# The down product in three products of halves, for 46 chunks of the last five expert stages

## The chip, the core and the metric

The kernel runs on one core of a Trainium2 chip. The metric is the device time of one execution in microseconds, as the median of several runs; lower is better. A core has TensorE (PE in the profile; its weight loads are PEld), VectorE (DVE), ScalarE (ACT), GpSimd (POOL) and SyncE (SP), which here issues all DMAs. Each engine works through its own queue in the order in which the program issues it; semaphores tie the queues together.

## The reference

Four rows of 1024 tokens with 128 features pass four residual sublayers: a gated linear attention (sublayer 1), a mixture of experts (MoE), a windowed softmax attention over 64 keys, and the same mixture of experts again. The part that the change touches is the MoE:

```python
logits = x @ gate_w.T                    # x: layernormed, 128 features
probs = softmax(logits)                  # 32 experts, top 8 of them, renormalised: comb
for each expert e:                       # 64 hidden features each
    g, u = split(x @ gate_up_w[e].T)
    out += (u * silu(g)) @ down_w[e].T * comb[:, e]
```

## The kernel before, in words

**Stages and chunks.** The MoE of 512 tokens is one stage. There are 16 stages: four rows, twice two halves (f is 0 or 1 for the first MoE, 2 or 3 for the second). A stage goes through the 32 experts in 16 chunks of two experts, 128 hidden features by 512 tokens each. The list SCHEDULE has the order of the stages and of the softmax attentions between them; a place in it has a name ("first", "second", ...). In this text the last five stages are called A, B, C, D and E, and the chunk 13 of stage A is A13:

- A is (row 2, f 2), place "second"; B is (3, 1), "third"; then half an attention; C is (2, 3), "fourth"; the other half; D is (3, 2), "second"; E is (3, 3), "fourth", the last. The stage ahead of A is (3, 0), "first".

**A chunk on the engines.** TensorE makes the gate product (three products of halves, float32r: hi x hi, hi x lo, lo x hi; lines 1489 to 1491) and then the up product in the same way, each into a PSUM bank of its own. ScalarE takes the silu of the gate bank into a tile of `work` (line 1030). VectorE multiplies it with the up bank, into the same tile (1270; "mul" below). GpSimd multiplies it with the tokens' weights for these two experts (847; "weigh"), which a DMA has spread over the partitions in `spread_w`. TensorE then adds the float32 product with the down weights to one bank (1512; "down"); the profile counts it as two matmuls.

**Order.** In slot s of a stage TensorE issues gate_up(s), down(s - 3) (LAG is 3), then the steps that a plan (PLAN, SPECIAL) names for the slot. ScalarE issues silu(s) and the slot's steps, VectorE mul(s) and the steps, GpSimd weigh(s) and the steps. The steps belong to other parts of the work: norms (m_stats and s_stats on VectorE, m_rstd and s_rstd on GpSimd, m_apply and s_apply on ScalarE), the transpose and its halves (moe_turn, z_hi, z_lo), the router (route and r_sum, top, weigh's exponentials on ScalarE, comb, cnorm, weighT), keys, queries, values, y_back, proj.

**Banks.** Gate and up products use three banks each, in the order of RINGS (line 378). A product waits until the chunk that last used its bank is done with it: the gate product for silu, the up product for mul. In stages that stand alone or in pairs behind an attention the ring has places where the bank comes back after two chunks instead of three: [0, 1, 2, 1, 2, 0, 1, 2, 0, 1, 2, 1, 2, 0, 1, 2] in C; in D and E positions 12 and 13 take the banks of 10 and 11.

**Weights.** `weighT` in slot 13 ends a stage's router work for the next one; ScalarE copies the result, SyncE sends it to DRAM and spreads it back by quarters of four chunks (two DMAs each) into the two halves of spread_w; the first waits for this chain, later ones for GpSimd to be done with the quarter two before.

Of the kernel before, what the change touches and what calls it, by code (L numbers as in the profile page):

```python
# [27 lines left out]
P = 128  # L28
# [32 lines left out]
HOOKS = 3  # L61
HALF_BLOCKS = NB * HG // 2
# [14 lines left out]
def own(*steps):  # L77
    return [(name, n, 0) for name, n in steps]


def back(*steps):
# [199 lines left out]
    },  # L281
    (ROWS - 1, "third"): {
# [88 lines left out]
for _, stage_place, stage_row, stage_part in SCHEDULE:  # L371
# [3 lines left out]
    else:  # L375
# [3 lines left out]
         48: [0, 1, 2] * 16, 64: ([0, 1, 2] * 6 + [1, 2]) * 2 + [0, 1, 2] * 8}  # L379
STARTS = [k for k, part in enumerate(SEGMENT) if k == 0 or SEGMENT[k - 1] != part]  # L380
# [40 lines left out]
def hybrid_block(nc, x, wqkv_a, lam, g1, g2, g3, w1, w2, wqkv_b, wout, bout, wgate, wg, wu, wd, out):  # L421
# [3 lines left out]
    with ExitStack() as ctx:  # L425
# [3 lines left out]
        def sem(name):  # L429
# [31 lines left out]
        qkv = sb("qkv", [P, T, 3 * D])  # L461
        elu = sb("elu", [P, T, 2 * D])
        kv_terms, w_terms = sb("kv_terms", [P, 2, HD * HD * H]), sb("w_terms", [P, H * HD * HD])
        kv = sb("kv", [P, HD * HD])
        attn, squares = sb("attn", [P, G, T, D]), sb("squares", [P, T, D])
# [3 lines left out]
        gain = sb("gain", [P, T, D])  # L469
# [25 lines left out]

        bank = [ctx.enter_context(nc.psum_tensor(f"bank{i}", [P, 512], F32))[:] for i in range(8)]
# [22 lines left out]
            sem("kv_terms_ready"), sem("kv_summed"), sem("w_terms_ready"), sem("attn_summed"))  # L519
        squared, tok_summed, head_gain, head_scaled = (  # L520
# [202 lines left out]
        def _(pool):  # L723
# [115 lines left out]
            def hidden(row, f, s):  # L839
                n = chunk(row, f, s)  # L840
                if n < EACH:
                    pool.wait_ge(spread_first[n], 32)
                elif s % EACH == 0:
                    k = n // EACH
                    pool.wait_ge(spread_loaded[k % 2], 32 * ((k + 1) // 2))
                pool.wait_ge(gated_ready, n + 1)
                pool.tensor_tensor(work[:, n % WORK], work[:, n % WORK],  # L847
                                   spread_w[:, n // EACH % 2, s % EACH], ALU.mult).then_inc(hid_gated, 1)
# [38 lines left out]
        def _(act):  # L887
# [147 lines left out]
            steps = {"x_apply": lambda row, n: norm_apply(row, "x", n), "m_apply": lambda row, n: norm_apply(row, "m", n),  # L1035
# [23 lines left out]
            for period, place, row, f in SCHEDULE:  # L1059
                if place not in PARTS:  # L1060
                    for s in range(CH):
                        if s == LAG and not starts_stream(row, f):
                            y_copy(STAGE_AT[row, f] - 1)
                        if s >= (1 if STAGE_AT[row, f] else FIRST) or not starts_stream(row, f):
                            silu(row, f, s)
                        run_steps(steps, period, place, s)
                else:
                    exponentials(row, f[0], 0)
                    exponentials(row, f[0], 1)
                    end, drain = END_AT[row, f[0]], HOOKS * (f[1] - f[0])  # L1070
# [20 lines left out]
        def _(dve):  # L1091
# [181 lines left out]
            steps = {"x_stats": lambda row, n: norm_stats(row, "x", n), "m_stats": lambda row, n: norm_stats(row, "m", n),  # L1273
# [84 lines left out]
        def _(pe):  # L1358
# [109 lines left out]
            def gate_up(row, f, s):  # L1468
# [10 lines left out]
                for w_hi, w_lo, banks, freed, ready in ((gate_hi, gate_lo, GATE_BANKS, silu_ready, gate_ready),  # L1479
                                                        (up_hi, up_lo, UP_BANKS, gated_ready, up_ready)):  # L1480
                    if there is not None:
# [22 lines left out]
            def down(n):  # L1504
                (row, f), c = STREAM[n // CH], n % CH
                pe.wait_ge(hid_gated, n + 1)
# [5 lines left out]
                pe.matmul(bank[Y_BANK], down_w[:, c], work[:, n % WORK], start=(c == 0),  # L1512
                          stop=(c == CH - 1)).then_inc(down_done, 1)
# [133 lines left out]
```

## Time and profile before

| | us |
|---|---|
| timed runs | 1011.54, 1008.63, 1011.01 |
| median | 1011.01 |
| profiled execution | 1018.66 |
| its span, first to last instruction | 1016.9 |
| mean granted TensorE clock | 0.956 |

The profile tells of one execution. Its span is the time from the first instruction to the last, and the rows give times in us from its start. "Busy" is the time in which an engine executes; a matmul's end is modelled, and matmuls that follow each other overlap in the rows, so that their pace is the distance between two starts. In a timeline a row has start, duration, engine, line, operation, what it writes and reads, the shape, how many were merged, and, in brackets, how long the engine had been idle and what released it.

### The profile page before, as it was taken

Reading aid. Unit: us, or ns where it says so; the run is one execution under the profiler, and the core shown is the slowest. Engines: PE = TensorE matmul, PEld = TensorE weight load, DVE = VectorE, ACT = ScalarE, POOL = GpSimd, SP = SyncE. Lnnn points to the kernel's source line nnn. Section 1 sums busy time; section 2 is a strip of 40 time slices with the busy share of each in tenths; the row PEclk is TensorE's granted clock in tenths of the full one; section 3 lists DMA queues with packets and bytes.
Section 4 is the critical chain, followed back from the end, with each engine's and each line's share of the span. In section 5 each row is a group of like instructions: output and inputs, shape, how many; then the busy total and the mean of one; then the engine's idle time right before and its main releaser. Section 6 shows DMA issues by size and latency. Waiting matters only on the chain.

```text
span 1016.9 us, 16679 instructions
## 1 busy us (share of the span) xinstructions
PE 917.2 (90%) x5472; PEld 629.8 (62%) x5472; DVE 643.8 (63%) x1447; ACT 612.5 (60%) x1876; POOL 660.4 (65%) x610
## 2 busy tenths in 40 slices
PE   2366999899999999899999899999999998998998
PEld 1144656676666666587666556677666566666665
DVE  4877865687759647688739636778744247447432
ACT  4444756984664576876674566698465458376432
POOL 6676967566778749556759746756665446545654
PEclk8558999999999999979999999999999999999999
DMA  5004361114453544510433544530344661260362
GB/s 181 0 1 97 82 127 44 43 44 101 92 125 85 128 92 90 132 38 17 94 85 86 124 90 89 124 83 17 70 100 86 125 142 39 63 147 13 83 127 62
DMA packets 63320, 85.67 MB, mean 84 GB/s; under 512 B 3777, under 2 KB 29186, under 8 KB 62978
## 3 DMA queue, kind: packets, MB, share of 16 engines
q1 hardware_dynamic: 63234, 84.61, 36.8%
q8 instruction: 43, 0.70, 0.3%
q14 instruction: 43, 0.35, 0.1%
HBM read 79.32 MB, written 5.28 MB: 83 GB/s over the span
## 4 chain that ended last, share of the span: by engine, by line
PE 58%; ACT 14%; POOL 8%; DVE 7%; issue 5%; DMA 1%; DVEq 0%; SPq 0%; ACTq 0%; POOLq 0%
PE bank L1512 16%; PE bank L1489 8%; PE bank L1491 8%; PE bank L1490 8%; ACT probs L1055 6%; PE bank L1533 3%; POOL work L847 3%; PE bank L1548 3%; PE bank L1562 2%; POOL kv_terms L812 2%; ACT work L1030 1%; PE bank L1526 1%; POOL probs L855 1%; PE bank L1372 1%; PE bank L1366 1%
## 5 line engine op out<-in xcount | busy, mean ns | idle before, releaser
L847 POOL TENSOR_TENSOR work<-work,spread_w 128x512 f32<-128x512 f32 x256 | 338.3, 1333 | 179.8 <-DVE work L1270 155.6
L1270 DVE TENSOR_TENSOR work<-work,bank 128x512 f32<-128x512 f32 x256 | 174.4, 682 | 227.9 <-ACT work L1030 143.3
L1512 PE MATMUL bank<-work,down_w 128*128 128x512 f32 x512 | 266.1, 604 | 14.2 <-POOL work L847 9.1
L1030 ACT ACTIVATE work<-bank 128x512 f32<-128x512 f32 x256 | 150.9, 595 | 182.3 <-PE bank L1491 179.3
L1055 ACT ACTIVATE probs<-bank,neg_max 128x96 f32<-128x96 f32 x512 | 166.0, 383 | 12.3 <-DVE neg_max L1298 6.5
L1489 PE MATMUL bank<-z_hi,gate_hi 128*128 128x512 f32 x256 | 169.0, 660 | 2.5 <-ACT work L1030 1.8
L855 POOL TENSOR_TENSOR probs<-probs,prob_inv 128x768 f32<-128x768 f32 x64 | 94.1, 1470 | 73.0 <-DVE prob_inv L1306 73.0
L1055 ACT ACTIVATION_READ_ACCUMULATOR probs<-bank,neg_max 128x1 f32 x512 | 126.8, 250 | 0.0
L1512 PEld LDWEIGHTS bank<-work,down_w 128*128 128x128 f32 x512 | 95.6, 191 | 44.4 <-POOL work L847 14.5
L1491 PE MATMUL bank<-z_hi,gate_lo 128*128 128x512 f32 x256 | 102.1, 399 | 0.0
L1491 PE MATMUL bank<-z_hi,up_lo 128*128 128x512 f32 x256 | 101.8, 398 | 0.0
L1489 PE MATMUL bank<-z_hi,up_hi 128*128 128x512 f32 x256 | 101.8, 398 | 0.0
L1490 PE MATMUL bank<-z_lo,gate_hi 128*128 128x512 f32 x256 | 101.6, 397 | 0.0
L1490 PE MATMUL bank<-z_lo,up_hi 128*128 128x512 f32 x256 | 100.9, 394 | 0.0
L812 POOL TENSOR_TENSOR kv_terms<-elu,qkv 128x1024 f32<-128x1024 f32 x32 | 81.6, 2553 | 17.9 <-DVE elu L1127 14.8
L1312 DVE COPY probsT<-bank 96x512 f32<-96x512 f32 x128 | 80.3, 666 | 5.0 <-PE bank L1548 4.7
L1298 DVE TENSOR_REDUCE neg_max<-bank 128x4 f32<-128x384 f32 x128 | 64.9, 548 | 24.7 <-PE bank L1533 23.7
L1548 PE MATMUL bank<-ident,probs 128*96 128x128 f32 x512 | 71.4, 282 | 10.2 <-DVE probsT L1312 8.4
L1489 PEld LDWEIGHTS bank<-z_hi,gate_hi 128*128 128x128 f32 x256 | 49.1, 192 | 40.2 <-issue 30.5
L1533 PE MATMUL bank<-keysT,qm 32*128 32x96 f32 x1024 | 70.7, 273 | 0.0
L1490 PEld LDWEIGHTS bank<-z_lo,gate_hi 128*128 128x128 f32 x256 | 49.3, 193 | 34.1 <-issue 31.3
L1548 PEld LDWEIGHTS bank<-ident,probs 128*96 128x96 f32 x512 | 54.2, 128 | 23.0 <-issue 13.3
(154 smaller groups left out, 1481.0 us busy)
## 6 DMA issues: line engine op xcount, KB each, us to landing
spread_w<-comb_dram SPq DMA_DIRECT2D x126, 512.0 KB, 6.7
vals<-v_dram SPq DMA_DIRECT2D x16, 384.0 KB, 4.0
x_buf<-x SPq DMA_DIRECT2D x8, 256.0 KB, 3.2
v_dram<-v_tok SPq DMA_DIRECT2D x8, 256.0 KB, 5.0
out<-xs SPq DMA_DIRECT2D x8, 256.0 KB, 4.2
spread_w<-wg SPq DMA_DIRECT2D x1, 1024.0 KB, 7.2
spread_w<-wu SPq DMA_DIRECT2D x1, 1024.0 KB, 9.3
comb_dram<-combT SPq DMA_DIRECT2D x16, 64.0 KB, 1.6
```

The source lines that it names most:

```text
L812: pool.tensor_tensor(kv_terms[:, i % 2].rearrange("p (e d h) -> p e d h", e=HD, d=HD), k.unsqueeze(2).broadcast_to([P, HD, HD, H]), v.unsq ...
L847: pool.tensor_tensor(work[:, n % WORK], work[:, n % WORK], spread_w[:, n // EACH % 2, s % EACH], ALU.mult).then_inc(hid_gated, 1)
L855: pool.tensor_tensor(pr, pr, prob_inv[:, i % 2, part].unsqueeze(2).broadcast_to([P, HALF_BLOCKS, KW]), ALU.mult).then_inc(probs_normed, 1)
L1030: act.activation(work[:, n % WORK], bank[GATE_BANKS[ring_of(row, f, s)]], ACT.Silu).then_inc(silu_ready, 1)
L1055: a = act.activation(probs[:, i % 2, m], bank[hg][:, b * KW:(b + 1) * KW], ACT.Exp, bias=neg_max[:, i % 2, m:m + 1], accum_out=prob_sum[:, ...
L1270: dve.tensor_tensor(work[:, n % WORK], work[:, n % WORK], bank[UP_BANKS[ring_of(row, f, s)]], ALU.mult).then_inc(gated_ready, 1)
L1489: pe.matmul(dst, w_hi[:, cols], h, start=True, stop=False)
L1490: pe.matmul(dst, w_hi[:, cols], l, start=False, stop=False)
L1491: pe.matmul(dst, w_lo[:, cols], h, start=False, stop=True).then_inc(ready, 1)
L1512: pe.matmul(bank[Y_BANK], down_w[:, c], work[:, n % WORK], start=(c == 0), stop=(c == CH - 1)).then_inc(down_done, 1)
L1533: mm = pe.matmul(bank[hg][:, KW * b:KW * (b + 1)], qm[feats, i // T, NB * (i % T) + b].rearrange("p j q -> p (j q)"), keysT[feats, first:f ...
L1548: mm = pe.transpose(bank[4 + b % 2][0:KW, P * hg:P * (hg + 1)], probs[:, i % 2, hg * NB + b], ident[:])
```

## The change

For 46 chunks in A to E (table PARTED) the down product is made like the gate and up products, of halves. GpSimd weighs silu's output as soon as silu is done. VectorE multiplies the weighed tile with the up bank and writes the result into the up bank. ScalarE copies the bank to `hid_hi` (float32r), VectorE subtracts it from the bank into `hid_lo`. Both are issued one chunk later in their queues: hi(s - 1) behind silu(s), lo(s - 1) behind mul(s), ahead of the slot's steps. TensorE adds three products, and the next product in that up bank waits for lo in place of mul. The down weights are split once, in the stage ahead of A. The new tiles lie where sublayer 1 had its own, which is through by then.

```diff
+PARTED = {
+    (2, 2): (2, 3, 5, 6, 8, 11, 13, 15),
+    (3, 1): (0, 2, 3, 6, 7, 8, 11, 12),
+    (2, 3): (2, 4, 6, 7, 8, 10, 12),
+    (3, 2): (3, 5, 6, 8, 11, 13, 14, 15),
+    (3, 3): (0, 1, 2, 3, 4, 5, 6, 7, 8, 9, 10, 11, 12, 13, 14),
+}
+PARTED_RING = 3
 SPECIAL:
+    (ROWS - 1, "first"): {
+        **PLAN["first"],
+        1: own(("h_red1", 1), ("down_hi", 0)),
+        7: back(("z_lo", 2)) + own(("down_lo", 0)),
+        10: back(("weigh", 2)) + own(("down_lo", 1)),
+    },
 GpSimd, hidden():
-                pool.wait_ge(gated_ready, n + 1)
+                if n in PARTED_AT:
+                    pool.wait_ge(silu_ready, n + 1)
+                else:
+                    pool.wait_ge(gated_ready, n + 1)
 ScalarE:
+            def down_hi_step(row, n):
+                act.wait_ge(kv_summed, ROWS * TILES)
+                act.activation(down_hi[:], down_w[:], ACT.Copy).then_inc(down_hi_ready, 1)
+            def hid_hi_step(row, f, s):
+                n = chunk(row, f, s)
+                j = PARTED_AT[n]
+                act.wait_ge(gated_ready, n + 1)
+                if j >= PARTED_RING:
+                    act.wait_ge(down_done, PARTED_CHUNKS[j - PARTED_RING] + 1)
+                act.activation(hid_hi[:, j % PARTED_RING], bank[UP_BANKS[ring_of(row, f, s)]],
+                               ACT.Copy).then_inc(hid_hi_ready, 1)
...
                             silu(row, f, s)
+                        if chunk(row, f, s) - 1 in PARTED_AT:
+                            hid_hi_step(*chunk_before(row, f, s))
                         run_steps(steps, period, place, s)
 VectorE, gated():
+                dve.wait_ge(up_ready, n + 1)
+                if n in PARTED_AT:
+                    up = bank[UP_BANKS[ring_of(row, f, s)]]
+                    dve.wait_ge(hid_gated, n + 1)
+                    dve.tensor_tensor(up, work[:, n % WORK], up, ALU.mult).then_inc(gated_ready, 1)
+                    return
...
+            def down_lo_step(row, n):
+                dve.wait_ge(down_hi_ready, 1)
+                part = slice(n * CH // 2, (n + 1) * CH // 2)
+                dve.tensor_tensor(down_lo[:, part], down_w[:, part], down_hi[:, part],
+                                  ALU.subtract).then_inc(down_lo_ready, 1)
+            def hid_lo_step(row, f, s):
+                j = PARTED_AT[chunk(row, f, s)]
+                dve.wait_ge(hid_hi_ready, j + 1)
+                dve.tensor_tensor(hid_lo[:, j % PARTED_RING], bank[UP_BANKS[ring_of(row, f, s)]],
+                                  hid_hi[:, j % PARTED_RING], ALU.subtract).then_inc(hid_lo_ready, 1)
...
                             gated(row, f, s)
+                        if chunk(row, f, s) - 1 in PARTED_AT:
+                            hid_lo_step(*chunk_before(row, f, s))
                         run_steps(steps, period, place, s)
 TensorE, gate_up():
-                    if there is not None:
+                    if there in PARTED_AT and banks == UP_BANKS:
+                        pe.wait_ge(hid_lo_ready, PARTED_AT[there] + 1)
+                    elif there is not None:
                         pe.wait_ge(freed, there + 1)
 TensorE, down(), a parted chunk (it waits for hid_lo_ready in place of hid_gated):
+                    hi, lo = hid_hi[:, j % PARTED_RING], hid_lo[:, j % PARTED_RING]
+                    pe.matmul(bank[Y_BANK], down_hi[:, c], hi, start=(c == 0), stop=False)
+                    pe.matmul(bank[Y_BANK], down_lo[:, c], hi, start=False, stop=False)
+                    pe.matmul(bank[Y_BANK], down_hi[:, c], lo, start=False, stop=(c == CH - 1)).then_inc(down_done, 1)
```

## Rows read from the trace of the kernel before

**Rows 1.** The page: busy time by engine; the chain that ended last

```profile
PE 917.2 (90%) x5472; PEld 629.8 (62%) x5472; DVE 643.8 (63%) x1447; ACT 612.5 (60%) x1876; POOL 660.4 (65%) x610
...
PE 58%; ACT 14%; POOL 8%; DVE 7%; issue 5%; DMA 1%; DVEq 0%; SPq 0%; ACTq 0%; POOLq 0%
```

**Rows 2.** Busy us by window: PE, PEld, DVE, ACT, POOL, then granted clock, DMA

```profile
804.46:806.48 2.02, 0.00 (x0) 0.00 (x0) 1.28 (x2) 0.59 (x2) 0.63 (x1) 1.00 1.08 216
806.48:811.30 4.82, 4.82 (x10) 2.90 (x11) 0.69 (x1) 2.91 (x5) 0.64 (x1) 0.65 0.17 31
980.00:1011.00 31.00, 31.00 (x112) 20.46 (x111) 9.64 (x14) 8.29 (x14) 19.10 (x15) 1.00 0.41 91
```

**Rows 3.** The timeline of chunk E2: from a down's start to the next

```profile
976.63 1.02 PE L1512 MATMUL bank<-work,down_w 128*128 128x512 f32 x2
...
977.72 0.39 PE L1490 MATMUL bank<-z_lo,gate_hi 128*128 128x512 f32 x1
...
978.18 0.40 PE L1489 MATMUL bank<-z_hi,up_hi 128*128 128x512 f32 x1
...
978.38 0.60 ACT L1030 ACTIVATE work<-bank 128x512 f32<-128x512 f32 x1 [1.64 <-PE bank L1491]
...
978.87 0.59 PE L1512 MATMUL bank<-work,down_w 128*128 128x512 f32 x1
```

**Rows 4.** Groups of instructions: busy us, mean ns of one, idle before and its releasers

```profile
L847 POOL TENSOR_TENSOR work<-work,spread_w 128x512 f32<-128x512 f32 x256 | 338.3, 1333 | 179.8 <-DVE work L1270 155.6 <-DMA spread_w<-comb_dram 23.1
L1270 DVE TENSOR_TENSOR work<-work,bank 128x512 f32<-128x512 f32 x256 | 174.4, 682 | 227.9 <-ACT work L1030 143.3 <-PE bank L1491 83.1 <-DVE x_buf L1213 0.9
L1030 ACT ACTIVATE work<-bank 128x512 f32<-128x512 f32 x256 | 150.9, 595 | 182.3 <-PE bank L1491 179.3
L1162 DVE TENSOR_TENSOR w_terms<-elu,kv 128x1024 f32<-128x1024 f32 x32 | 44.1, 1377 | 0.6
L1225 DVE TENSOR_TENSOR z_lo<-bank,z_hi 128x512 fp32r<-128x512 f32 x16 | 11.0, 685 | 5.1 <-ACT z_hi L981 5.1
L981 ACT ACTIVATE z_hi<-bank 128x512 fp32r<-128x512 f32 x16 | 9.6, 603 | 15.2 <-PE bank L1366 15.2
L1207 DVE TENSOR_TENSOR attn_sum<-attn,gain 128x512 f32<-128x512 f32 x8 | 6.8, 850 | 4.1 <-ACT gain L968 4.0
```

**Rows 5.** Timeline: weigh of B0; weighT ahead of E; weigh of E0

```profile
794.77 1.29 POOL L847 TENSOR_TENSOR work<-work,spread_w 128x512 f32<-128x512 f32 x1 [4.12 <-DMA spread_w<-comb_dram]
...
968.09 0.60 PE L1427 MATMUL bank<-ident,comb 128*32 128x128 f32 x4
...
978.55 1.28 POOL L847 TENSOR_TENSOR work<-work,spread_w 128x512 f32<-128x512 f32 x1 [4.07 <-DMA spread_w<-comb_dram]
```

**Rows 6.** Timeline: table load, silu of D11 and D12, comb, D13's up product

```profile
962.89 1.28 ACT L1030 ACT_TABLE_LOAD   x1
964.18 1.08 ACT L1030 ACTIVATE work<-bank 128x512 f32<-128x512 f32 x2
...
965.42 0.28 DVE L1253 SCALAR_TENSOR_TENSOR comb<-replaced,expd 128x128 f32<-128x128 f32 x1
...
966.54 0.39 PE L1489 MATMUL bank<-z_hi,up_hi 128*128 128x512 f32 x1
```

**Rows 7.** Timeline of B: B2's up product, the stats of slot 3, queries

```profile
797.83 0.40 PE L1489 MATMUL bank<-z_hi,up_hi 128*128 128x512 f32 x1
...
799.40 0.86 DVE L1113 BATCH_NORM_STATS2 stats<-xs 128x6 f32<-128x128 f32 x4
...
806.48 0.70 PE L1446 MATMUL bank<-seqT,qkv_b_w 128*128 128x512 f32 x1 [2.02 <-DVEq L1216]
```

**Rows 8.** Timeline: weigh(A13, A14), B0's up product, z_lo in C, weigh(D3, D4)

```profile
786.36 2.53 POOL L847 TENSOR_TENSOR work<-work,spread_w 128x512 f32<-128x512 f32 x2
...
789.80 0.40 PE L1489 MATMUL bank<-z_hi,up_hi 128*128 128x512 f32 x1
...
884.71 0.68 DVE L1225 TENSOR_TENSOR z_lo<-bank,z_hi 128x512 fp32r<-128x512 f32 x1
...
946.54 2.53 POOL L847 TENSOR_TENSOR work<-work,spread_w 128x512 f32<-128x512 f32 x2
```

More of the change, by code:

```diff
@@ L379 @@
          48: [0, 1, 2] * 16, 64: ([0, 1, 2] * 6 + [1, 2]) * 2 + [0, 1, 2] * 8}
+PARTED_CHUNKS = [STAGE_AT[stage] * CH + c for stage, chunks in PARTED.items() for c in chunks]
+PARTED_AT = {n: j for j, n in enumerate(PARTED_CHUNKS)}
+assert PARTED_CHUNKS == sorted(PARTED_CHUNKS)
 STARTS = [k for k, part in enumerate(SEGMENT) if k == 0 or SEGMENT[k - 1] != part]
@@ L460, in hybrid_block @@
         zT = sb("zT", [P, GT])
-        qkv = sb("qkv", [P, T, 3 * D])
-        elu = sb("elu", [P, T, 2 * D])
-        kv_terms, w_terms = sb("kv_terms", [P, 2, HD * HD * H]), sb("w_terms", [P, H * HD * HD])
         kv = sb("kv", [P, HD * HD])
-        attn, squares = sb("attn", [P, G, T, D]), sb("squares", [P, T, D])
         head_ms, head_rms = sb("head_ms", [P, T * H]), sb("head_rms", [P, T * H])
@@ L468, in hybrid_block @@
         tok_ms, tok_rms = sb("tok_ms", [P, T]), sb("tok_rms", [P, T])
-        gain = sb("gain", [P, T, D])
         attn_sum = sb("attn_sum", [P, T, D])
@@ L494, in hybrid_block @@
         mix_all = sb("mix_all", [P, NB * P])
+        with ExitStack() as first_sublayer:
+            kv_terms, qkv, elu, w_terms, squares, gain, attn = (
+                first_sublayer.enter_context(nc.sbuf_tensor(name, shape, F32)) for name, shape in (
+                    ("kv_terms", [P, 2, HD * HD * H]), ("qkv", [P, T, 3 * D]), ("elu", [P, T, 2 * D]),
+                    ("w_terms", [P, H * HD * HD]), ("squares", [P, T, D]), ("gain", [P, T, D]),
+                    ("attn", [P, G, T, D])))
+        down_hi, down_lo = sb("down_hi", [P, CH, D], F32R), sb("down_lo", [P, CH, D], F32R)
+        hid_hi, hid_lo = sb("hid_hi", [P, PARTED_RING, GT], F32R), sb("hid_lo", [P, PARTED_RING, GT], F32R)
         bank = [ctx.enter_context(nc.psum_tensor(f"bank{i}", [P, 512], F32))[:] for i in range(8)]
@@ L519, in hybrid_block @@
             sem("kv_terms_ready"), sem("kv_summed"), sem("w_terms_ready"), sem("attn_summed"))
+        down_hi_ready, down_lo_ready, hid_hi_ready, hid_lo_ready = (
+            sem("down_hi_ready"), sem("down_lo_ready"), sem("hid_hi_ready"), sem("hid_lo_ready"))
         squared, tok_summed, head_gain, head_scaled = (
@@ L555, in chunk, with chunk_before @@
             return STAGE_AT[row, f] * CH + s
+        def chunk_before(row, f, s):
+            return (row, f, s - 1) if s else (*STREAM[STAGE_AT[row, f] - 1], CH - 1)
         def group(row, g):
@@ L1033, in here @@
                 return lambda row, n: None if (row, name, n) in APART else copy(row, n)
-            steps = {"x_apply": lambda row, n: norm_apply(row, "x", n), "m_apply": lambda row, n: norm_apply(row, "m", n),
+            def down_hi_step(row, n):
[9 more added lines that the diff above has]
+                               ACT.Copy).then_inc(hid_hi_ready, 1)
+            steps = {"down_hi": down_hi_step,
+                     "x_apply": lambda row, n: norm_apply(row, "x", n), "m_apply": lambda row, n: norm_apply(row, "m", n),
                      "s_apply": lambda row, n: norm_apply(row, "s", n), "x_turn": x_turn, "qkv": qkv_step, "qkv_first": qkv_first,
@@ L1267, in gated @@
                 n = chunk(row, f, s)
+                dve.wait_ge(up_ready, n + 1)
[4 more added lines that the diff above has]
+                    return
                 dve.wait_ge(silu_ready, n + 1)
-                dve.wait_ge(up_ready, n + 1)
                 dve.tensor_tensor(work[:, n % WORK], work[:, n % WORK], bank[UP_BANKS[ring_of(row, f, s)]],
                                   ALU.mult).then_inc(gated_ready, 1)
-            steps = {"x_stats": lambda row, n: norm_stats(row, "x", n), "m_stats": lambda row, n: norm_stats(row, "m", n),
+            def down_lo_step(row, n):
[8 more added lines that the diff above has]
+                                  hid_hi[:, j % PARTED_RING], ALU.subtract).then_inc(hid_lo_ready, 1)
+            steps = {"down_lo": down_lo_step,
+                     "x_stats": lambda row, n: norm_stats(row, "x", n), "m_stats": lambda row, n: norm_stats(row, "m", n),
                      "s_stats": lambda row, n: norm_stats(row, "s", n), "lam": lam_step_coef, "elu": elu_step, "elu_first": elu_of_first, "w_hi": w_hi, "w_lo": w_lo, "kvsum": kvsum, "wterm": wterm, "wred": wred,
@@ L1505, in down @@
                 (row, f), c = STREAM[n // CH], n % CH
-                pe.wait_ge(hid_gated, n + 1)
+                if n in PARTED_AT:
+                    pe.wait_ge(hid_lo_ready, PARTED_AT[n] + 1)
+                else:
+                    pe.wait_ge(hid_gated, n + 1)
                 if c == 0:
@@ L1511, in down @@
                         pe.wait_ge(mix_taken, tile(after[0], after[2]))
-                pe.matmul(bank[Y_BANK], down_w[:, c], work[:, n % WORK], start=(c == 0),
-                          stop=(c == CH - 1)).then_inc(down_done, 1)
+                if n in PARTED_AT:
+                    j = PARTED_AT[n]
+                    if j == 0:
+                        pe.wait_ge(down_lo_ready, 2)
+                    hi, lo = hid_hi[:, j % PARTED_RING], hid_lo[:, j % PARTED_RING]
+                    pe.matmul(bank[Y_BANK], down_hi[:, c], hi, start=(c == 0), stop=False)
+                    pe.matmul(bank[Y_BANK], down_lo[:, c], hi, start=False, stop=False)
+                    pe.matmul(bank[Y_BANK], down_hi[:, c], lo, start=False, stop=(c == CH - 1)).then_inc(down_done, 1)
+                else:
+                    pe.matmul(bank[Y_BANK], down_w[:, c], work[:, n % WORK], start=(c == 0),
+                              stop=(c == CH - 1)).then_inc(down_done, 1)
             def score(row, i, pair):
```

## The prediction

> **What bounds the kernel now.** I read the page's busy shares and its chain first: TensorE is busy 90% of the span, and 58% of the chain that ended last is its own [rows 1]. Then busy time by window: from 980 to 1011 us TensorE works in all 31.00 us, at full clock, while GpSimd is busy 19.10, VectorE 9.64 and ScalarE 8.29 [rows 2]. Then the timeline of one chunk in stage E, without other steps in it: its pace is 978.87 - 976.63 = 2.24 us, and every microsecond is a product [rows 3]. So TensorE sets the end in stages A to E, wherever nobody is late for it; the question is what its shorter work is worth when more work of the other three engines has to arrive in time.
>
> **What TensorE saves.** From the start of a down product to the second gate product of the next chunk is 977.72 - 976.63 = 1.09 us; products of halves follow each other by (978.18 - 977.72) / 2 = 0.23 us. So the float32 product takes 1.09 - 0.23 = 0.86 us [rows 3]. Three products of halves take 3 x 0.23 = 0.69. Saved: 0.17 us a chunk, 46 x 0.17 = 7.8 us at most. The weight loads of halves lie beside products already.
>
> **What is added.** Per parted chunk one ScalarE copy (hi; as z_hi, 603 ns) and one VectorE subtract (lo; as z_lo, 685 ns). The multiply (mul) now writes into PSUM, which no row shows; nearest are 682 ns (PSUM in, SBUF out) and 850 ns (both in SBUF) [rows 4]. I take 0.69. Once: the copy of the down weights, 4 x 595 = 2.4 us of ScalarE, and two VectorE subtracts of 1024 columns at 1.38 each. They stand in the stage ahead of A, where ScalarE and VectorE have room of that size and LAG hides a late chunk: I take 0; with the cover gone all of it is 2.4 + 2.8 = 5.2 us.
>
> **The new chain of a chunk.** Count from u, the start of its first up product. Silu starts at u + 0.20 [rows 3] and ends u + 0.80; weigh (1.29) ends u + 2.16, mul u + 2.92, hi u + 3.6. In VectorE's queue lo(n) stands behind mul(n+1). If n+1 is parted too, mul(n+1) waits for its own weigh and ends 2.08 later, at u + 5.0; lo then ends at u + 5.75. The up bank, held to there now, is wanted by chunk n+3 at u + 3 x 2.08 = 6.24. So in bare stretches 0.5 us is left, and the saving is real; were mul and lo 0.16 slower each, it would be 0 and still no stall. But whatever delays silu, weigh or mul of a parted chunk, or of the one behind it, comes out in TensorE once it is over 0.5 us. Before, mul did not wait for GpSimd, and the down product three chunks later (u + 7) had some 4 us of room. I followed the queues of the four engines through the stages by the rows' durations. The largest places:
>
> 1. *E0.* Its weights land late: GpSimd idles 4.07 us and starts at 978.55, which is 10.1 us after weighT ends on TensorE (968.09 + 0.36) [rows 5]. Covered before; now mul(E0) waits for it, and lo(D15) is queued behind mul(E0): 978.55 + 1.29 + 0.07 + 0.69 + 0.05 + 0.69 + 0.06 = 981.4 for the up bank of E2. TensorE wants it at 978.18 [rows 3], less 0.5 saved by the downs of D11, D13 and D14 since weighT: 977.7. Stall 3.7.
> 2. *D11.* Its silu is late, at 964.18, behind the reload of the table after weigh's exponentials. Now: silu to 964.78, weigh 966.1, mul 966.9, then the three operations of comb (0.28, 0.29, 0.18, with gaps 0.9) and mul(D12), 968.5, lo 969.3. D13 uses the same bank (the ring of 32 goes back two chunks there) and wanted it at 966.54 [rows 6]. Stall 2.8.
> 3. *B3.* The stats of slot 3 started 1.57 us after u of B2 (799.40 - 797.83), and the chain stats, rstd, m_apply, silu(B5), mul(B5), y_back, queries already kept TensorE idle for 2.02 us [rows 7]. They now stand behind mul(B3) and lo(B2): u + 5.75. GpSimd, which freed its rstd later than the stats, gives back a part; with the delay that B enters with I get 2.1 more.
> 4. *A13, A15, B0.* weigh(A13) starts at 786.36, behind s_rstd [rows 8], whose stats stand behind lo(A11): 788.5. mul 790.5, then mul(A14) and lo(A13) to 792.0; B0's up product wanted 790.3: 1.75. Beside it cnorm behind hi(A11) keeps weighT back 0.9, z_lo behind lo(A6) the router 0.4, lo(A2) 0.3. weigh(B0) waits 4.12 us for its weights as in place 1 [rows 5] and holds lo(A15); keys waits 0.7 for the copy behind hi(A15). From 789.80 [rows 8] and on, B2's up product comes 2.9 us later than now, savings deducted.
>
> The ledger, net of savings, in us late against now: at B2 +2.9; behind B's queries +5.0 (place 3); at the end of B +5.75 (z_lo behind lo(B6) 0.85, cnorm behind hi(B11) 1.1, savings 1.2). C: lo(C2) 0.8 (bank reused two on), z_lo, now at 884.71 [rows 8], behind weigh(C7), mul(C7) and lo(C6) 1.8, lo(C10) behind the late mul(C11) 1.4, savings and rest -1.0: +8.75. D: lo(D3), whose weigh starts at 946.54 behind rstd [rows 8], 0.6; m_apply behind hi(D3), hence lo(D5), 1.0; router 0.55; place 2 2.85; savings 0.7: +13.05. E: 3.65 at E2, savings 0.5 ahead of it, then 13 x 0.17 = 2.2 for E's own downs and 0.2 at the last chunk, whose weigh takes over: **+13.8 us**.
>
> **The clock.** While TensorE idles 2.02 us the granted clock is 1.00; in the 4.82 us behind it it is 0.65, a mix of its two levels, 2.4 and 1.2 GHz [rows 2, 7]. That stretch holds queries (0.86), gate and up (1.39) and a down (0.86), 3.1 us at full clock: a fall costs 1.7. B's idle is there already; D11's (2.8) and E0's (3.7) are new and as long. By the row both would fall: +3.4; nothing says that they must at another phase, so I take half, +1.7, and keep both ends. The Trainium skill (TensorE: Matmul & The Clock Gate, HAM oscillation — how this bites in real kernels) says that a wait long enough between bursts puts the array back to its low clock and that it has to earn the high one again. By that rule the second and third new stall cost more than their length, 3.4 us in all; without it the sum is 13.8. This trace agrees for the one gap named.
>
> **Sum.** 13.8 + 1.7 = 15.5. The profiled execution took 1018.66 us (span 1016.9) and would take 1034.2; it stands 7.65 above the median of the three timed runs, 1011.01, so the median becomes **1026.5 us**, 1.5% slower.
>
> **Rivals.**
> - *Only the hard stalls are real.* My following adds many waits of 0.3 to 1.8 us, and any slack that I overlook takes them away. What remains are places 1, 2 and 3, whose waits are each a queue order plus a row: 3.4 + 2.5 + 1.9 = 7.8 against 7.8 saved: 1011 us, no change to +3.
> - *Faster.* TensorE saves 7.8 us and the stalls stay under that. Price: place 1 vanishes if the weights of E0 land 3.7 us sooner relative to TensorE, and place 2 if silu(D11) doesn't wait for the table. For it: the bare chunks have 0.5 us of room, and E has most of the parted chunks. Against: the row of 4.07 us idle. With 5 us of stalls kept: 1011.0 - 2.8 = 1008; with none, 1003.
> - *VectorE's write into PSUM is slow.* If mul takes over 0.85 + 0.3, the slack of 0.5 in bare stretches is gone too, and E loses up to 0.4 in each of 13 chunks: 1026.5 + 5 = 1031.5. The subtract of z_lo (PSUM in) at 685 speaks against it.
> - *The change doesn't shorten the down product,* three starts or weight loads eating 0.17: then all stalls and no saving, 1026.5 + 7.8 = 1034. The six products of halves at 0.23 each speak against it.
>
> **Chances.** Forecast (1018 to 1031) 0.60; hard stalls alone 0.17; faster 0.10; slow write 0.08; no saving 0.05. A difference under 0.3% (3 us) can't be told from none. Of the second case a third is no change and little is faster. Faster 0.11, same 0.08, slower 0.81. The range 1009 to 1032 leaves out most of the faster case, the last one and the far end of the third; the forecast's own is 1018 to 1031.
>
> **What would show it.** Right: gaps of TensorE before the first up product of E2 (about 3.5 us, with GpSimd's wait for spread_w ahead and mul, mul, lo behind) and of D13 (2.8); the wait before queries in B near 4 us; three products of 0.23 in the down's place; low clock after one or both new gaps; bare chunks of E at 2.08. Wrong: weigh(E0) starting less than 7 us after weighT; no gap at E2 or D13; a pace in E over 2.1 (mul, hi or lo dearer than their rows); a stall in the stage ahead of A over 1 us.

## The result, and the profile after

The changed kernel takes 1029.65 us (median of 4 runs, 1028.82 to 1031.78); the kernel before, beside it on the same chip, takes 1009.97 (4 runs, 1008.63 to 1011.54). The ratio is 1.0187, with a 95% interval of 1.0156 to 1.0217: 1.9% slower. The forecast was 1026.5 us. One run of the kernel before beside experiments 4 and 5 took 1331.99 us at a granted clock of 0.645, and their medians leave it out.

The page, as [rows 1] shows it of before (busy time by engine; the chain that ended last):

```profile
PE 911.4 (89%) x5518; PEld 634.6 (62%) x5518; DVE 669.6 (65%) x1495; ACT 637.0 (62%) x1923; POOL 660.7 (64%) x610
...
PE 48%; ACT 16%; POOL 10%; DVE 9%; issue 6%; DMA 3%; SPq 0%; DVEq 0%; ACTq 0%; POOLq 0%
```

TensorE is busy 5.8 us less, in a span that is 11.4 us longer (1028.3, execution 1030.02). Its share of the chain fell from 58% to 48%. VectorE is busy 25.8 us more and ScalarE 24.5, GpSimd the same.

The groups, as in [rows 4] (busy us, mean ns of one | idle before and its releasers). First VectorE's multiply into the up bank, then its subtract lo, ScalarE's copy hi, and the three products:

```profile
L1317 DVE TENSOR_TENSOR bank<-work,bank 128x512 f32<-128x512 f32 x46 | 32.0, 696 | 87.4 <-POOL work L876 83.6 <-PE bank L1558 3.8
L1332 DVE TENSOR_TENSOR hid_lo<-bank,hid_hi 128x512 fp32r<-128x512 f32 x46 | 31.5, 684 | 0.3
L1074 ACT ACTIVATE hid_hi<-bank 128x512 fp32r<-128x512 f32 x46 | 27.5, 597 | 33.1 <-DVE bank L1317 32.0
L1587 PE MATMUL bank<-hid_hi,down_hi 128*128 128x512 f32 x46 | 18.7, 407 | 0.2 <-DVE hid_lo L1332 0.2
```

The multiply into PSUM took 696 ns, so the price that no row of before showed is no surprise. It idled 83.6 us for GpSimd's weigh: that is the wait which VectorE's queue didn't have before. The chunk in stage E, as in [rows 3]:

```profile
1004.18 0.39 PE L1556 MATMUL bank<-z_hi,up_hi 128*128 128x512 f32 x1
...
1004.87 0.40 PE L1587 MATMUL bank<-hid_hi,down_hi 128*128 128x512 f32 x1
...
1005.57 0.39 PE L1556 MATMUL bank<-z_hi,gate_hi 128*128 128x512 f32 x1
...
1006.27 0.39 PE L1556 MATMUL bank<-z_hi,up_hi 128*128 128x512 f32 x1
```

Three products fill 1005.57 - 1004.87 = 0.70 us, and the pace is 2.09 against 2.24 before. The part of the edit that shortens TensorE's work does that. What TensorE waits for in stages A to E (us in total, times, longest):

```profile
PE bank L1556 <- DVE hid_lo L1332: 10.0, 7, 3.5
PE bank L1511 <- DVEq L1261: 4.2, 1, 4.2
...
PE bank L1492 <- ACT comb L1021: 1.9, 2, 1.3
PE bank L1482 <- DVE z_lo L1270: 1.4, 2, 1.2
```

The first row is the up product of a later chunk, waiting for the bank that lo still reads. The second is queries in B, the third weighT, the last the router in C. The two largest waits of the first row, in D and E (timeline of every engine; chosen lines), answer to [rows 6] and [rows 5]:

```profile
966.90 1.28 ACT L1059 ACT_TABLE_LOAD   x1
968.19 1.08 ACT L1059 ACTIVATE work<-bank 128x512 f32<-128x512 f32 x2
968.87 1.27 POOL L876 TENSOR_TENSOR work<-work,spread_w 128x512 f32<-128x512 f32 x1 [1.15 <-ACT work L1059]
970.24 0.70 DVE L1317 TENSOR_TENSOR bank<-work,bank 128x512 f32<-128x512 f32 x1 [3.90 <-POOL work L876]
970.85 0.29 DVE L1298 SCALAR_TENSOR_TENSOR comb<-replaced,expd 128x128 f32<-128x128 f32 x1
...
972.17 0.68 DVE L1332 TENSOR_TENSOR hid_lo<-bank,hid_hi 128x512 fp32r<-128x512 f32 x1
972.91 0.50 PE L1556 MATMUL bank<-z_hi,up_hi 128*128 128x512 f32 x1 [2.35 <-DVE hid_lo L1332]
...
986.86 2.49 POOL L876 TENSOR_TENSOR work<-work,spread_w 128x512 f32<-128x512 f32 x2 [5.24 <-DMA spread_w<-comb_dram]
988.22 0.69 DVE L1317 TENSOR_TENSOR bank<-work,bank 128x512 f32<-128x512 f32 x1 [5.22 <-POOL work L876]
988.83 0.68 DVE L1332 TENSOR_TENSOR hid_lo<-bank,hid_hi 128x512 fp32r<-128x512 f32 x1
989.57 0.50 PE L1556 MATMUL bank<-z_hi,up_hi 128*128 128x512 f32 x1 [3.52 <-DVE hid_lo L1332]
```

Table, silu, weigh, mul, comb, mul, lo, and only then D13's up product; weights from the DMA, weigh, mul of E0, lo of D15, and only then E2's. The windows (busy us of PE, PEld, DVE, ACT, POOL, then granted clock, DMA) of the waits in B, C, D and E, each with the stretch behind it, as [rows 2]:

```profile
799.22:803.41 4.19, 0.01 (x2) 0.00 (x1) 1.29 (x2) 2.13 (x5) 2.30 (x4) 0.93 0.53 106
803.41:807.41 4.00, 4.00 (x10) 2.55 (x11) 0.00 (x0) 1.89 (x4) 0.63 (x1) 0.65 0.00 0
...
885.75:886.95 1.20, 0.00 (x1) 0.01 (x1) 1.14 (x2) 0.58 (x1) 1.20 (x1) 1.00 0.44 108
886.95:892.00 5.05, 5.05 (x21) 4.24 (x22) 3.23 (x9) 1.09 (x2) 0.71 (x2) 0.66 0.87 184
970.56:972.91 2.35, 0.00 (x0) 0.00 (x0) 2.23 (x6) 1.81 (x6) 0.51 (x1) 1.00 0.01 3
972.91:977.50 4.59, 4.59 (x13) 2.79 (x14) 0.69 (x1) 0.81 (x2) 1.99 (x2) 0.63 0.02 5
986.05:989.57 3.52, 0.00 (x1) 0.01 (x1) 1.35 (x3) 0.62 (x2) 2.49 (x2) 1.00 1.08 212
989.57:994.00 4.43, 4.43 (x12) 3.50 (x13) 2.45 (x4) 2.69 (x5) 1.64 (x2) 0.61 0.13 25
```

In this execution each of the four waits, the one of 1.20 us too, goes with 3.4 us at half clock, which makes the mean of 0.61 to 0.66 in the stretches behind them; before, only the wait in B did [rows 2].

**How two executions are compared.** Ahead of A both kernels do the same but for the copy of the down weights, yet in the two traces A0's first up product starts at 750.80 and 743.94 us. The clock goes with it: between 100 and 740 us the execution before stood at the half clock for 20.5 us in all, the one after for 6.8 (summed over the slices of the trace). The copy of the down weights costs nothing that shows: from the first up product of the stage ahead of A to A0's is 46.6 us in both. So I count each chunk's first up product from A0's, and give the difference to the same count before. In us late:

| kernel | B0 | B2 | B7 | C3 | D2 | D12 | D14 | E1 | E2 | E4 | E15 | end |
|---|---|---|---|---|---|---|---|---|---|---|---|---|
| after | 1.5 | 2.0 | 3.7 | 4.9 | 9.4 | 10.7 | 15.0 | 14.7 | 18.3 | 19.6 | 17.9 | 18.2 |
| products alone | -0.9 | -1.1 | -1.4 | 2.2 | 1.3 | 0.7 | 0.7 | 0.4 | 0.3 | -0.1 | -1.8 | -1.9 |
| chain alone | 2.4 | 2.8 | 5.7 | 8.3 | 11.6 | 13.2 | 15.7 | 15.7 | 18.7 | 20.4 | 20.5 | 20.7 |
| E0 whole | 1.5 | 2.2 | 5.0 | 6.3 | 9.3 | 10.6 | 14.9 | 14.6 | 14.5 | 17.3 | 15.6 | 15.9 |
| E0 to E3 whole | 1.6 | 2.1 | 4.7 | 5.9 | 8.9 | 10.2 | 14.5 | 14.2 | 14.0 | 13.9 | 12.7 | 13.0 |
| D11 whole | 1.6 | 2.0 | 4.9 | 6.1 | 9.1 | 10.4 | 10.4 | 10.3 | 13.5 | 15.9 | 14.2 | 14.5 |
| B2, B3 whole | 1.5 | 2.1 | 2.1 | 3.4 | 6.3 | 7.3 | 11.6 | 11.3 | 14.1 | 13.9 | 12.2 | 12.6 |
| lo first | 4.1 | 5.1 | 8.6 | 9.4 | 15.5 | 18.3 | 22.3 | 22.0 | 21.8 | 25.7 | 24.0 | 25.1 |
| 29 chunks | -0.3 | -0.3 | -1.5 | 0.3 | 1.8 | 1.4 | 1.5 | 1.3 | 1.2 | 1.0 | -0.2 | 0.9 |
| 22 chunks | -0.5 | -0.5 | -1.5 | -1.7 | -1.9 | -2.1 | -2.1 | -2.2 | -2.4 | -2.5 | -3.7 | -3.4 |
| before again | 0 | 0 | -1.1 | -1.1 | -1.1 | -1.1 | -1.1 | -1.1 | -1.1 | -1.1 | -1.1 | -1.1 |

So the change costs 18.2 us behind A0 in this pair; the medians differ by 19.7.

Up to its last microseconds the kernel before had one clock fall behind A0, in B; the changed one has that and three more. What each of the three costs shows against the other traces of the changed chain. In C, from C8 to D2, 3.9 us are lost with the fall and 2.3 to 2.4 in the four traces of experiments 2 and 3, which have the same wait of 1.2 us there and no fall: 1.5 us. From D13 to D14, where no parted product lies, 1.8. From E2 to E4, 1.4 are lost here and 0.2 gained in the B2, B3 trace, without a fall: 1.6. Together 4.9 us.

### The profile page after: what moved, and what is told of

Its sections match the earlier page's. It is cut to its first block, busy times and chain, and to the rows that moved or that the text cites. A ratio compares the mean times of both kernels' runs of the same rounds, so it can differ in the third digit from the quotient of the medians.

```text
span 1028.3 us, 16910 instructions
## 1 busy us (share of the span) xinstructions
PE 911.4 (89%) x5518; PEld 634.6 (62%) x5518; DVE 669.6 (65%) x1495; ACT 637.0 (62%) x1923; POOL 660.7 (64%) x610
## 4 chain that ended last, share of the span: by engine, by line
PE 48%; ACT 16%; POOL 10%; DVE 9%; issue 6%; DMA 3%; SPq 0%; DVEq 0%; ACTq 0%; POOLq 0%
PE bank L1591 11%; PE bank L1556 6%; ACT probs L1098 6%; PE bank L1558 6%; PE bank L1557 6%; POOL work L876 5%; PE bank L1612 3%; PE bank L1627 3%; DMA spread_w<-comb_dram 2%; ACT work L1059 2%; PE bank L1641 2%; DVE work L1320 1%; POOL kv_terms L838 1%; ACT L1059 1%; PE bank L1605 1%
## 5 line engine op out<-in xcount | busy, mean ns | idle before, releaser
L1320 DVE TENSOR_TENSOR work<-work,bank 128x512 f32<-128x512 f32 x210 | 142.8, 681 | 140.9 <-ACT work L1059 117.2
L1591 PE MATMUL bank<-work,down_w 128*128 128x512 f32 x420 | 218.8, 604 | 13.3 <-POOL work L876 7.9
L1556 PE MATMUL bank<-z_hi,gate_hi 128*128 128x512 f32 x256 | 158.8, 620 | 3.5 <-ACT elu L969 2.0
L1591 PEld LDWEIGHTS bank<-work,down_w 128*128 128x128 f32 x420 | 78.0, 191 | 38.9 <-POOL work L876 13.1
L838 POOL TENSOR_TENSOR kv_terms<-elu,qkv 128x1024 f32<-128x1024 f32 x32 | 81.5, 2549 | 17.0 <-DVE elu L1172 13.8
L1317 DVE TENSOR_TENSOR bank<-work,bank 128x512 f32<-128x512 f32 x46 | 32.0, 696 | 87.4 <-POOL work L876 83.6
L1627 PE MATMUL bank<-ident,probs 128*96 128x128 f32 x512 | 69.6, 278 | 10.2 <-DVE probsT L1375 8.4
L1557 PEld LDWEIGHTS bank<-z_lo,gate_hi 128*128 128x128 f32 x256 | 49.7, 194 | 28.7 <-issue 24.5
```

The source lines that it names most:

```text
L838: pool.tensor_tensor(kv_terms[:, i % 2].rearrange("p (e d h) -> p e d h", e=HD, d=HD), k.unsqueeze(2).broadcast_to([P, HD, HD, H]), v.unsq ...
L1556: pe.matmul(dst, w_hi[:, cols], h, start=True, stop=False)
L1557: pe.matmul(dst, w_hi[:, cols], l, start=False, stop=False)
L1627: mm = pe.transpose(bank[4 + b % 2][0:KW, P * hg:P * (hg + 1)], probs[:, i % 2, hg * NB + b], ident[:])
```

## The experiments

In all but the last, the kernel is the changed one with the edit that is shown. "Whole" is a chunk whose down product stays one float32 product, in the old order. The kernel before was timed beside each experiment, the changed one only beside the first pair above; a difference to its 1029.65 us is therefore best taken through the ratios.

**1. TensorE's part alone and the chain alone.** The first writes the halves once and lets every parted down product read those, so that the result leaves out these chunks' hidden values; the multiply, weigh and the bank's release stand as before. The second does all the new work but reads `work` with one float32 product, which leaves out the up half of these chunks. Each cut of the code is marked with three dots.

```
# products alone
+        15: own(("halves_once", 0)),
...
-                if n in PARTED_AT:
-                    pe.wait_ge(hid_lo_ready, PARTED_AT[n] + 1)
-                else:
-                    pe.wait_ge(hid_gated, n + 1)
+                pe.wait_ge(hid_gated, n + 1)
...
-                    hi, lo = hid_hi[:, j % PARTED_RING], hid_lo[:, j % PARTED_RING]
+                    hi, lo = hid_hi[:, 0], hid_lo[:, 0]
# chain alone
-                    pe.matmul(bank[Y_BANK], down_hi[:, c], hi, start=(c == 0), stop=False)
...
+                    pe.matmul(bank[Y_BANK], down_w[:, c], work[:, n % WORK], start=(c == 0),
+                              stop=(c == CH - 1)).then_inc(down_done, 1)
```

> Of the change only TensorE's part is kept: 46 down products are three products of halves, but of two tiles that are written once in the stage ahead of A (4 us of waiting chunks at most), so the chain silu, mul, weigh and all waits and banks are those of the kernel before. The down products of these chunks do not use the hidden values. Theory Q (each product of halves takes 0.23 us, what is lost is queueing): 46 x 0.167 = 7.7 us less than before, of which up to 1.5 us can get lost where TensorE waits anyway (B's queries, the attentions): 1002.5 to 1004, and bare chunks of E at 2.08 us. Theory W (the three products bring nothing, or contention makes them dearer): 1008 to 1012 and E at 2.2 or more.

> The other half alone: weigh on silu, mul into the up bank, hi, lo and all waits for them as in the changed kernel, but the down product is one float32 product of 0.86 us (of the weighed silu, without the up half, so its values are not those of the reference). Theory Q: the stalls of the changed kernel stay (its 19.7 us more plus its 7.7 us saved = 27 us of stalls and slow clock), a little less since slower downs give the chain 0.17 us more of room a chunk and hide some of the smaller ones: 1032 to 1037. Theory W (the loss is in the products themselves): 1012 or less.

Products alone: 1009.49 us (median of 10, 1002.48 to 1012.62) against 1011.64 (13 runs), ratio 0.9962 (0.9934 to 0.9989). That is 2.1 us where some 6 to 7.7 were expected: a miss, and by the time alone it is Theory W's. Theory W's other half, a pace in E of 2.2 or more, didn't come. The trace tells why this execution's end shows so little: TensorE saves almost as forecast (B15 is 2.1 early; E1 to E15 gain 2.2 in 14 chunks; the pace in E is 2.08), but in attention at 831 us stands a half-clock stretch of 13.65 us which no other trace has, and behind it C3 is 4.3 later than B15. Without that the end would be 6 us early.

The ten timed runs part in the same way. Four have a mean granted clock of 0.962 to 0.964 and take 1002.48 to 1006.47 us; six have 0.954 to 0.959 and take 1009.40 to 1012.62. Of the kernel before, beside them, six have 0.962 to 0.964, at 1008.04 to 1010.76. At a like clock the products save some 4.5 us. Why more runs of this kernel have a low clock than of the kernel before is not shown.

Chain alone: 1033.47 (4 runs, 1030.56 to 1036.25), ratio 1.0216 (1.0174 to 1.0258), as expected. The two parts, -0.4% and +2.2%, give 1.8%; together they measured 1.9%. So the loss is the new chain's, and the products give a part of it back. In the trace of the chain alone the clock doesn't fall behind the wait before D13 (2.20 us) and falls behind the one before E2 (2.80).

**2. The wait before E2.**

```
-    (3, 3): (0, 1, 2, 3, 4, 5, 6, 7, 8, 9, 10, 11, 12, 13, 14),
+    (3, 3): (1, 2, 3, 4, 5, 6, 7, 8, 9, 10, 11, 12, 13, 14),      # E0 whole
+    (3, 3): (4, 5, 6, 7, 8, 9, 10, 11, 12, 13, 14),               # E0 to E3 whole
```

> The changed kernel with chunk 0 of E left as before (float32), so that mul(E0) no longer waits for the weights that land late, and lo(D15), behind it, neither. Theory Q: the wait of 3.7 us before E2's up product goes, and with it the fall of the clock that followed (1.7 us); 0.17 of saving is given up: 5 us less than the changed kernel, 1024 to 1025.5. Rival L (lo(D15) is late for its own sake: weigh, mul and hi of D15 in a row): the wait stays over 2 us, 1028 or more.

> The changed kernel with chunks 0 to 3 of E left as before, not E0 alone. With E0 alone whole the wait before E2's up product went (0.85 us of idle and pace lost there in place of 3.5), but 2.8 us were lost between E2 and E4. Theory Q (four weighs stand in a row behind the late weights, and any of the four that is parted is late): nothing is lost between E1 and E4 now, and E runs 0.17 a chunk faster from E7 on. Rival S (the steady chain of consecutive parted chunks does not keep up at its start): the loss moves on behind E4.

E0 whole: 1028.6 (4 runs, 1024.84 to 1031.48), ratio 1.0166 (1.0121 to 1.021): a miss by 3 us of its median. Two runs at a mean clock of 0.963 took 1024.84 and 1026.01 us, close to what was expected; two at 0.956, the profiled one among them, took 1031.19 and 1031.48. E2's wait is gone (E1 to E2 -0.15 instead of +3.53), yet 2.8 are lost between E2 and E4. Its waits of TensorE have a new row, and the timeline (chosen lines) names the queue:

```profile
PE bank L1591 <- ACT yT L1090: 2.7, 1, 2.7
```

```profile
990.35 3.75 POOL L876 TENSOR_TENSOR work<-work,spread_w 128x512 f32<-128x512 f32 x3 [5.34 <-DMA spread_w<-comb_dram]
...
993.71 0.60 ACT L1074 ACTIVATE hid_hi<-bank 128x512 fp32r<-128x512 f32 x1 [3.63 <-DVE bank L1317]
994.21 0.59 ACT L1090 ACTIVATE yT<-bank 128x512 f32<-128x512 f32 x1
...
994.94 1.10 PE L1591 MATMUL bank<-work,down_w 128*128 128x512 f32 x2 [2.72 <-ACT yT L1090]
```

The late weights now hold mul and hi of E1; in ScalarE's queue the copy that frees the y bank stands behind hi, and E's first down needs that bank. One cause, another queue. With E0 to E3 whole, taken once (1028.6 us, span 1026.9), nothing is lost from E1 to E4 (-0.3) and the row is gone: 5.2 us at the end against the change, as expected. Of these 0.5 lie ahead of E (D14), the rest in it, its clock fall included. The time of that execution doesn't show it, because its A0 starts 3.8 us later than the changed kernel's.

**3. The waits before D13 and in B.**

```
+    (3, 2): (3, 5, 6, 8, 13, 14, 15),      # D11 whole
+    (3, 1): (0, 6, 7, 8, 11, 12),          # B2, B3 whole
```

> The changed kernel with chunk 11 of D left as before. Theory Q: D13's up product no longer waits for lo(D11); 2.5 us and the fall of the clock behind it (1.7) go, 0.17 is given up: 4 us less than the changed kernel, 1025 to 1026.5. Rival T (the reload of ScalarE's table for silu holds TensorE anyway, through the gate bank or through cnorm and weighT): at most 1.5 us less, 1028 or more.

> The changed kernel with chunks 2 and 3 of B left as before. Theory Q: the stats of slot 3 are 2 us earlier, and TensorE's wait before B's queries is 2 to 2.5 us in place of 4.2. Rival A (the wait comes with B's late start, behind s_apply and hi(A15)): it stays over 3.5 us.

D11 whole: 1029.93 (4 runs, 1026.97 to 1031.12), ratio 1.0177 (1.0141 to 1.0213). By its median nothing changed: a miss, 3.4 us above what was expected, and the time that Rival T gave. But Rival T's reason isn't there. In the trace, which is of the fastest of the four, D13's wait is gone with the clock fall behind it: D12 to D14 lose 0.0 instead of 4.3, and 3.7 are left at the end. Two of its falls, in B and at E2's wait, are 6.8 us long instead of 3.4, and the mean clocks of the four runs are 0.952 to 0.957, against 0.953 to 0.960 of the changed kernel; so the clock may have taken back what the wait gave, which isn't shown for the three runs without a trace.

B2 and B3 whole, one execution (1020.99 us, span 1019.2): the wait before queries is 2.2 instead of 4.2,

```profile
PE bank L1511 <- DVEq L1261: 2.2, 1, 2.2
```

and B7 1.6 earlier, as expected. At the end 5.6 us less are lost than with the change; the other 4 are for the most part two falls of the clock, in C and behind E2, which this execution doesn't have. Its E2 waits 2.85 us, by the same chain, and the clock doesn't fall (the wait, and the stretch behind it):

```profile
979.21:982.06 2.85, 0.00 (x1) 0.00 (x1) 1.35 (x3) 0.62 (x2) 2.48 (x2) 1.00 1.07 211
982.06:986.50 4.44, 4.44 (x19) 3.64 (x20) 2.46 (x4) 2.75 (x5) 2.59 (x2) 1.00 0.19 34
```

**4. The order in VectorE's queue.** If lo(n) stood ahead of mul(n+1), the bank would be free about 1.5 us sooner, at u + 4.3 instead of u + 5.8 by the expectation's count.

```
+    if chunk(row, f, s) - 1 in PARTED_AT:
+        hid_lo_step(*chunk_before(row, f, s))
     if s >= (1 if STAGE_AT[row, f] else FIRST) or not starts_stream(row, f):
         gated(row, f, s)
-    if chunk(row, f, s) - 1 in PARTED_AT:
-        hid_lo_step(*chunk_before(row, f, s))
```

> The changed kernel with one order turned round: VectorE issues lo(s - 1) ahead of mul(s), not behind it; all 46 chunks stay. Theory Q (what costs is that lo stands in the queue behind a mul that now waits for GpSimd): lo of a chunk ends at u + 4.3 us in place of u + 5.8. E2's wait of 3.5 us goes (lo(D15) no longer behind mul(E0)), but the late weights then hold lo(E0), and E3 waits about 2 us; B0's 1.2 us before its up product goes; D13's wait falls from 2.4 to about 1.6, since comb is still ahead; B's queries about 0.7 less. Sum 5 to 8 us less than the changed kernel: 1022 to 1025. Rival H (what costs is that mul waits for GpSimd at all, and ScalarE's hi holds silu back): less than 2 us, 1028 or more.

It is 1040.28 (4 runs, 1033.77 to 1042.93), ratio 1.0278 (1.0241 to 1.0316): a clear miss, of the wrong sign. (The profiled execution is the fastest of the four, 6.5 us below their median.) What VectorE waits for in A to E:

```profile
DVE bank L1317 <- POOL work L876: 62.7, 24, 6.6
DVE hid_lo L1332 <- ACT hid_hi L1074: 29.7, 38, 2.5
```

lo now waits 29.7 us for hi, where it idled 0.3 before: hi stands behind the next silu in ScalarE's queue. VectorE spends that time idle, and its other steps come later: z_lo keeps TensorE waiting 5.7 us instead of 1.4. The wait before E2 is gone (E1 to E2 -0.15), but 3.9 us are lost between E2 and E4, a clock fall included. lo behind mul was the better order.

**5. Fewer chunks.** First, in the order of experiment 4, A 5, 6, 8, 15; B and C 6, 8, 12; D 5, 6, 8, 13 to 15; E 2 to 14 (29 chunks). Then, in the change's order, those alone behind whose mul and lo no step in the queues was late:

```
+    (2, 2): (5, 6, 8),
+    (3, 1): (8, 12),
+    (2, 3): (8, 12),
+    (3, 2): (8, 13, 14, 15),
+    (3, 3): (4, 5, 6, 7, 8, 9, 10, 11, 12, 13, 14),
```

> A version from the reasons found: lo ahead of mul, and only those chunks parted that no slow step, late weights or short bank reuse touches: A 5, 6, 8, 15; B 6, 8, 12; C 6, 8, 12; D 5, 6, 8, 13, 14, 15; E 2 to 14; 29 chunks. Theory Q: 29 x 0.167 = 4.8 us saved, up to 1.5 of it lost in B's queries, the last chunk and small waits: 3.3 to 4.8 us faster than the kernel before (0.3 to 0.5%), no new fall of the clock. Rival H (parting costs wherever it is done, by ScalarE's and VectorE's extra work): no faster than before, or slower.

> lo stands behind mul again (turned round it held VectorE until ScalarE's hi, itself behind a silu, was through: 1040 us). Parted are the 22 chunks behind which no profile so far showed a loss: A 5, 6, 8; B 8, 12; C 8, 12; D 8, 13, 14, 15; E 4 to 14. Theory Q: 22 x 0.167 = 3.7 us saved from A to E, 0.3 of it lost at the last chunk, so E15's up product is 3 to 3.7 us earlier, counted from A0, than in the kernel before, and no wait of TensorE before an up product is over 0.3 us; in the medians that is 0.3%, on the edge of what can be told: 1007.5 to 1010. Rival H (parting costs wherever it is done): E15 is not over 1.5 us earlier. Rival G (as the 29 chunks of the last try, whose stages A to E came out level in the profile while its median stood 0.6% above: something outside the waits, the clock's falls, makes it slower): E15 over 3 us earlier, but the median at 1011 or more with a mean clock under the other's.

29 chunks: 1017.33 (median of 12) against 1011.38 (16 runs), ratio 1.0058 (1.0039 to 1.0078), another miss. Its trace is nearly level with before at the end (+0.9), with losses at z_lo (0.8), at the last down (1.0) and of 1.5 us in the attention ahead of C, where a half-clock stretch stands. That explains why it gains nothing, and not the 6 us of the medians; the rest lies outside what this trace shows, and its runs have mean clocks of 0.953 to 0.963, against 0.956 to 0.966 before. 22 chunks: 1010.49 (median of 12, 1006.47 to 1014.14) against 1012.4 (17 runs), ratio 0.9982 (0.9963 to 1.0001). In its trace no up product waits for hid_lo (one down does, for 0.2 us), and E15 comes 253.2 us behind A0, against 256.9 before and 255.9 in the next run. The first difference, 3.7, has the cost of B's clock fall in it, which this trace doesn't have; the next run doesn't have it either, so that 2.6 us are the parted chunks' own, a little under the 3 that were expected. By the times alone it is not told apart from no change; 22 x 0.17 = 3.7 us is the whole that could come.

**6. The kernel before once more.** Unchanged, for the spread of one execution.

> The kernel before once more, for a second profile of it: the first one took 1018.66 us, 7 more than its median. If the clock's falls ahead of A make the difference (20.5 us at the lower clock between 100 and 740 us there, 3.4 to 7 in most other profiles), this one has fewer of them and A0's up product about 0.5 us earlier for each us less; the stages A to E take the same time within 0.5 us.

1016.48 us (span 1014.8), again 4 above the median. The expectation came out in part. Between 100 and 740 us this execution has not fewer but more half-clock time, 23.9 us against 20.5, and A0 still stands 1.1 us earlier, at 749.72. So half a microsecond for each is only rough: a stretch at 222 us costs 1.2 us of TensorE's time, of which 0.9 are gone again at 239 us. A to E repeat within 0.02 us but for one place: behind queries' 2.02 us wait the clock stayed at 1.00, and everything from there is 1.1 earlier.

```profile
803.20:805.36 2.16, 0.18 (x2) 0.00 (x0) 1.28 (x2) 0.77 (x2) 0.60 (x1) 1.00 1.05 213
805.36:809.50 4.14, 3.75 (x14) 2.21 (x15) 0.00 (x0) 2.91 (x5) 0.67 (x1) 1.00 0.12 21
```

## Why the prediction was right

The direction, the mechanism and the size held: 1029.65 stands inside the forecast's own range (1018 to 1031), 3.15 us over its value. Step by step, forecast and then measured:

- *TensorE's saving.* 0.17 a chunk; E4 to E15 gain 1.70 in 11 chunks, 0.155. Bare chunks stay clean, as the slack of 0.5 us said. The rivals of a slow write (696 ns) and of no saving fall.
- *Splitting the down weights.* Taken at nothing; the stage ahead of A takes 46.6 us with it and without it.
- *A and the entry of B.* +2.9 at B2; measured +2.0. B0's loss is there (1.35), some of the smaller ones beside it are not.
- *Place 3, queries.* A wait of 4.1; measured 4.2 (the second row of the waits above, against 2.02 in [rows 7]). Behind it +5.0; measured +3.7, short by what B2 was short, and a little more.
- *End of C.* +8.75; measured +9.4 at D2, of which 1.5 is clock: 7.9 without it.
- *Place 2, D13.* 2.8; measured 2.35 of wait, 2.5 lost. *Place 1, E2.* 3.7; measured 3.52. In both, the row before the change and the queue order gave the size. Behind D13 the ledger said +13.05; D14's 15.0 less the clock's 1.5 and 1.8 is 11.7.
- *The sum without the clock.* +13.8. Measured 18.2, less the three new falls (1.5 in C, 1.8 behind D13, 1.6 behind E2), is 13.3. That it comes so near is in part luck: the ledger was 1.3 too high behind D13, and in E it counted 0.2 us as saved at the last chunk, where 0.3 were lost, and 0.17 a chunk where 0.155 came.
- *The clock.* This is the term that was mis-sized: +1.7, with 3.4 as its far end; in the profiled execution it was 4.9. Two falls came where two new waits were forecast, at 1.8 and 1.6 us each as priced (though B's fall, from which the price was read, costs 1.1 by the kernel before once more). A third came with C's wait of 1.20 us, which the ledger had as a delay and not as a risk for the clock; the four traces with the same wait in experiments 2 and 3 have no fall there. Taking half was too little, as the other traces show. Over the twelve traces, all eight waits of TensorE in A to E of 3.27 us and more have a half-clock stretch that starts in them or within 2.1 us of their end; of the seventeen of 1.98 to 2.85 us eleven have one, D13's in five traces of six. Among the six without are E2's of 2.85 us in experiment 3 and B's of 2.02 in the kernel before once more, where the same wait in the first execution has one. So 3.4 would have been the nearer guess, and the sum 17.2. The rule cited in the prediction (the Trainium skill, TensorE: Matmul & The Clock Gate, HAM oscillation — how this bites in real kernels) names the right effect and sign. By these runs its price is paid in some executions and not in others, for the same wait.
- *From a profiled time to the median.* The 7.65 us by which the profiled execution stood above the median were carried over as a constant. By the traces it is for the most part half-clock stretches ahead of A, which differ from one execution to the next. The changed kernel's own profiled execution has fewer and stands 0.4 from its median. So the forecast for the profiled execution, 1034.2, was missed (1030.02), while the one for the median held.

The rival of hard stalls alone (1011) is refuted: places 1 to 3 lost 3.5, 2.5 and about 2 us, and the many small ones about 12 more: 13.3 net of the clock, plus 46 x 0.155 = 7.1 saved, less 8.0. It is they that decide the sign. These 12 us are a remainder; no experiment took the small waits away one by one, but the 22 chunks that leave them all out lose nothing.

What stays open: the ten runs with the products alone gain 2 us by their median, 4.5 at the same clock and 6 by the trace without its long stretch. The clock makes the difference between their fast and slow half; whether it falls more often because of the edit was not shown. The same holds for the medians of D11 whole and of the 29 chunks.

## What to carry over

Before an operation is moved into a chain, list what stands behind it in its engine's queue, and behind each engine that the chain now passes: here 7.1 us of saved products were paid with some 20 us of late work on TensorE's side, and with 4.9 us of clock falls on top. An order that takes a wait away from one queue puts it into another (E0 whole, lo first), so forecast the order of all queues and not the one wait. Spend such an edit only on chunks with nothing late behind them, and expect no more than their count times the saving. When such small differences are timed, read each run's mean clock beside its time.

## What the runs showed of the hardware

- Ahead of A the programs of all these traces are all but the same, and their single executions reach A0 at 740.5 to 752.6 us; most of that goes with the time at half clock. Half-clock time between 100 and 740 us, and A0's start: 3.4 us and 742.0 (chain alone), 6.8 and 743.9 (after), 13.6 and 747.9 (22 chunks), 20.5 and 750.8 (before), 23.9 and 749.7 (before again). From the first to the fourth that is 8.8 us for 17.1 of half clock, about half a us each. The fifth doesn't fit, nor do the 29 chunks, at 752.6 with 23.9 us as well.
- Behind 100 us most stretches are 3.4 us long, some 6.8, one in each of three traces 10.2 and one 13.65; one of 3.4 in A to E cost 1.1 to 1.8 us.
- VectorE writes a 128x512 multiply into PSUM in 696 ns and into SBUF, with an operand from PSUM, in 682 [rows 4].
